# One Trainium2 core: value products of a DMA-turned P one step later, q's products ahead of k's and v's

## The reference

```
q = (x_norm @ Wq.T)   32 heads of 128;   k, v = ctx @ Wk.T, ctx @ Wv.T   8 heads, each used by 4 of q's
q, k = rmsnorm(q) * wq, rmsnorm(k) * wk
scores = q k^T / sqrt(128) + mask;  P = softmax(scores);  out = (P v) @ Wo.T
x = x + tanh(g) * out
```

## Time and profile before

| | us |
|---|---|
| median of 3 runs | 1319.82 (1318.8 to 1320.96) |
| the profiled execution | 1320.3 |
| its span, first to last instruction | 1318.5 |
| TensorE busy in the span | 1302.9 (99%) |
| VectorE busy | 1001.4 (76%) |
| ScalarE busy | 867.4 (66%) |
| GpSimd busy | 621.9 (47%) |

### The profile page before, as it was taken

One profiled execution on the slowest core, in us unless ns is written; L12 is line 12 of the kernel. 1 busy time (PEld: TensorE's weight loads), 2 busy tenths in 40 slices (PEclk: granted clock), 3 DMA queues, 4 the chain that ended last, 5 costly groups with the idle time before them and its releaser, 6 DMA issues.

```text
span 1318.5 us, 25473 instructions
## 1 busy us (share of the span) xinstructions
PE 1302.9 (99%) x7477; PEld 1102.0 (84%) x7493; DVE 1001.4 (76%) x2106; ACT 867.4 (66%) x3356; POOL 621.9 (47%) x683
## 2 busy tenths in 40 slices
PE   8999999999999999999999999999999999999999
PEld 7888888888888888877777788888888888888887
DVE  6878787887878788688888858777767677677656
ACT  5767667676767776645566456777767767676551
POOL 2546566565656666446677533532323323332232
DMA  7011110211121121020301013532232222321101
GB/s 297 1 57 55 63 55 20 68 48 68 50 68 50 35 71 33 13 64 20 103 20 48 20 48 89 161 64 77 60 67 69 40 70 57 80 56 32 17 8 56
DMA packets 87340, 78.34 MB, mean 59 GB/s; under 512 B 70880, under 2 KB 75872, under 8 KB 83168
## 3 DMA queue, kind: packets, MB, share of 16 engines
q1 hardware_dynamic: 70272, 71.91, 18.6%
q10 hardware_dynamic: 16672, 4.46, 1.6%
q0 software_dynamic: 320, 1.05, 0.2%
HBM read 57.48 MB, written 3.15 MB: 46 GB/s over the span
## 4 chain that ended last, share of the span: by engine, by line
PE 76%; issue 8%; POOL 6%; DVE 5%; DMA 3%; ACT 1%; POOLq 0%; ACTq 0%; DVEq 0%; SPq 0%
PE bank L1298 54%; PE bank L1362 6%; PE bank L1290 6%; PE bank L1393 6%; PE bank L1324 2%; DMA p_turned<-p_planes 2%; POOL w_lo L551 2%; POOL rstd L580 2%; PE bank L1479 1%; PE bank L1379 1%; POOL fw_y L591 1%; POOL fw_y L589 1%; DVE probs L1138 1%; ACT squares L769 1%; DMA ctx_raw<-in_ctxT 0%
## 5 line engine op out<-in xcount | busy, mean ns | idle before, releaser
L551 POOL TENSOR_TENSOR w_lo<-w_raw,w_hi (+1 forms) x150 | 192.8, 1303 | 164.7 <-ACT w_hi L730 164.7
L769 ACT ACTIVATE squares<-bank 128x128 bf16<-128x128 f32 x512 | 134.4, 278 | 184.7 <-PE bank L1298 184.5
L711 ACT ACTIVATE probs<-probs,negmax 128x128 f32<-128x128 f32 x512 | 198.2, 391 | 7.1 <-DVE negmax L1010 4.5
L576 POOL TENSOR_TENSOR meansq<-sumsq,scalars 128x5 f32<-128x5 f32 x128 | 27.5, 215 | 354.1 <-ACT squares L769 354.1
L580 POOL TENSOR_TENSOR rstd<-meansq,scalars 128x5 f32<-128x5 f32 x128 | 153.2, 1197 | 10.7 <-POOL meansq L576 1.1
L1298 PE MATMUL bank<-w_hi,oT_hi 128*128 (+1 forms) x512 | 150.9, 416 | 0.0
L1298 PE MATMUL bank<-w_hi,xT_hi 128*128 (+1 forms) x512 | 140.3, 395 | 0.0
L1298 PE MATMUL bank<-w_lo,xT_hi 128*128 (+1 forms) x512 | 138.1, 390 | 0.3
L1362 PEld LDWEIGHTS bank<-kT,qT 128*128 128x128 f32 x1024 | 131.7, 191 | 7.7
L1298 PE MATMUL bank<-w_hi,oT_lo 128*128 (+1 forms) x512 | 138.0, 391 | 0.0
L1298 PE MATMUL bank<-w_lo,oT_hi 128*128 (+1 forms) x512 | 137.6, 390 | 0.0
(11 more groups left out here) (129 smaller groups left out, 3073.1 us busy)
## 6 DMA issues: line engine op xcount, KB each, us to landing
w_raw<-in_wq SPq DMA_DIRECT2D x16, 1024.0 KB, 4.8
w_raw<-in_wo SPq DMA_DIRECT2D x16, 1024.0 KB, 9.8
w_raw<-in_wkv SPq DMA_DIRECT2D x16, 512.0 KB, 5.6
fw_raw<-in_ffn_w SPq DMA_DIRECT2D x36, 192.0 KB, 2.3
x_sb<-in_x SPq DMA_DIRECT2D x7, 256.0 KB, 10.7
ctx_raw<-in_ctxT SPq DMA_DIRECT2D x7, 256.0 KB, 9.7
fw_raw<-in_ffn_w SPq DMA_DIRECT2D x7, 256.0 KB, 2.7
out<-x_sb SPq DMA_DIRECT2D x7, 256.0 KB, 2.0
```

The lines of the kernel that those rows point to most:

```text
L551: last = nc.gpsimd.tensor_tensor(lo, raw, hi.bitcast(FP32), ALU.subtract)
L576: nc.gpsimd.tensor_tensor(meansq[:, :], sumsq[:, :], eps_sb[:, :], ALU.add).then_inc(ms_done, 1)
L711: last = nc.scalar.activation(probs[:, h * P:(h + 1) * P], probs[:, h * P:(h + 1) * P], ACT.Exp, bias=negmax[:, h:h + 1], accum_out=rowsum ...
L769: last = nc.scalar.activation(squares[:, h // 2, (b + 1) % 4, h % 2, :], q_bank(n, kind)[:, h * P:(h + 1) * P], ACT.Square, scale=SCALE, a ...
```

## The change

`values_late` holds for steps 76 to 124. In these:

- TensorE makes q's products first, then the first 4 of the 12 products of k and v, then the value products of unit n-3 (`values(3)`, before: of n-2, behind kn's transpose), then the other 8. q's transposes follow kn's at once. Step 75 has no value products; step 124 has two sets.
- ScalarE squares q before k (into qn as a dump, so it waits for the transposes of the last qn), and writes oT_hi between the two. sq_done, for which GpSimd waits, comes with k's squares. In all steps by DMA, the placing of P's upper half and pT_hi go to the end of the step.
- VectorE makes pT_lo at the head of the next step (`whole_lower`), ahead of the planes; oT_lo comes behind the planes, behind the int4 work of steps 76 to 78, and behind wp_lo, which moves to steps 84 to 87. `place_lower` goes to the end of the step. In step 124 the moments and the normalising of the last layer's first tile come earlier.
- SPLIT_ZONE gives step 81 two pieces (before: three), step 82 two (two), step 83 two (one).

SP's order is unchanged, and on GpSimd only the pieces of steps 81 to 83 move.

The diff, cut to its core:

```diff
-              32: ((E + 1, 6), (E + 1, 7)), 33: ((E + 1, 8), (E + 1, 9), (E + 2, 0)), 34: ((E + 2, 1), (E + 2, 2)),
-              35: ((E + 2, 3),), 36: ((E + 2, 4), (E + 2, 5)), 37: ((E + 2, 6),), 38: ((E + 2, 7), (E + 2, 8)),
+              32: ((E + 1, 6), (E + 1, 7)), 33: ((E + 1, 8), (E + 1, 9)), 34: ((E + 2, 0), (E + 2, 1)),
+              35: ((E + 2, 2), (E + 2, 3)), 36: ((E + 2, 4), (E + 2, 5)), 37: ((E + 2, 6),), 38: ((E + 2, 7), (E + 2, 8)),
...
+        def values_late(n, kind):
+
+            return kind == PLAIN or (isinstance(n, int) and DMA0 < n <= DMA1)
...
+            def q_squares(n, b, kind):
+                act.wait_ge(q_ps, n + 1)
+                wait(act, rs_done, n)
+                if values_late(n, kind):
+                    act.wait_ge(qk_ps, n)
+                for h in range(REP):
...
                 if has(n, 0):
-
+                    if values_late(n, kind):
+                        q_squares(n, b, kind)
+                        output_upper(n)
                     act.wait_ge(kv_ps, n + 1)
...
+            def whole_lower(n):
+
+                dve.wait_ge(pt_hid, n - 2)
+                nc.vector.tensor_tensor(pT_lo[:, :], p_whole[:, :], pT_hi[:, :].bitcast(FP32),
+                                        ALU.subtract).then_inc(pt_lod, 1)
...
+                if by_dma(n, kind) or t.last == 0:
+                    scaled_probs(n)
+                if values_late(n, kind):
+                    whole_lower(n)
                 if by_dma(n, kind):
-                    scaled_probs(n)
                     probs_planes(n)
+                for k in gathered(n - 1, kind):
...
+                if kind == ZONE and 0 <= n - INT4_0 < INT4_PARTS and values_late(n, kind):
+                    int4_weights(n - INT4_0)
+                if values_late(n, kind):
+                    output_lower(n)
...
+                    if values_late(n, kind):
+                        queries()
+                        wait(pe, kT_sb, n)
+                        keys_values(slice(0, KT))
+                        values(3)
+                        keys_values(slice(KT, 3 * KT)).then_inc(kv_ps, 1)
```

More of the change, by code:

```diff
@@ L730, in split_upper, with output_upper @@
                     nc.scalar.activation(hi, raw, ACT.Copy).then_inc(split_hi, 1)
+            def q_squares(n, b, kind):
[4 more added lines that the diff above has]
+                for h in range(REP):
+                    dump = (qn[:, h * P // 2:(h + 1) * P // 2].bitcast(BF16) if values_late(n, kind)
+                            else squares[:, h // 2, (b + 1) % 4, h % 2, :])
+                    last = nc.scalar.activation(dump, q_bank(n, kind)[:, h * P:(h + 1) * P], ACT.Square, scale=SCALE,
+                                                accum_out=sumsq[:, h:h + 1])
+                return last
+            def output_upper(n):
+                act.wait_ge(pv_ps, n - 2)
+                wait(act, y_ps, n - 3)
+                nc.scalar.activation(oT_hi[:, :], psPO[:, :], ACT.Copy).then_inc(o_hid, 1)
             def step(n, b, kind, j, q=None):
@@ L734, in step @@
                 exp_late = calm(n, kind) or (kind == FIRST and b == BATCHES - 1)
[L735 to L739, removed]
+                if has(n, 3) and not values_late(n, kind):
+                    output_upper(n)
                 if calm(n, kind) or (kind == ZONE and n == FFN0):
@@ L764, in step @@
                     hidden_turned(0, t.down)
[L765 to L771, removed]
+                if has(n, 0) and not values_late(n, kind):
+                    q_squares(n, b, kind).then_inc(sq_done, 1)
                 if t.first is not None:
@@ L836, in step @@
                     nc.scalar.activation(qT[:, :], psSQ[:, :], ACT.Copy).then_inc(qT_sb, 1)
+                if has(n, 2) and by_dma(n, kind):
+                    act.wait_ge(pv_ps, n - 2)
+                    act.wait_ge(planes_turned, (n - DMA0 + 1) * 16)
+                    nc.scalar.activation(halves(p_whole[:, :])[:, :, 1], p_turned[:, 0:KT, :].rearrange("p k t -> p (k t)"),
+                                         ACT.Copy).then_inc(upper_placed, 1)
+                    act.wait_ge(upper_placed, n - DMA0 + 2)
+                    act.wait_ge(lower_placed, n - DMA0 + 2)
+                    nc.scalar.activation(pT_hi[:, :], p_whole[:, :], ACT.Copy).then_inc(pt_hid, 1)
                 if has(n, 1) and (t.next is not None or t.down is not None):
@@ L1096, in step @@
                     row_inverse(n)
-                if has(n, 2) and not t.active and not by_dma(n, kind):
+                if has(n, 2) and not t.active and not by_dma(n, kind) and t.last != 0:
                     scaled_probs(n)
@@ L1105, in step @@
                         ctx_lower(t.first)
-                if kind == ZONE and 0 <= n - INT4_0 < INT4_PARTS:
+                if kind == ZONE and 0 <= n - INT4_0 < INT4_PARTS and not values_late(n, kind):
                     int4_weights(n - INT4_0)
[L1108 to L1112, removed]
                 if t.first is not None:
@@ L1115, in step @@
                     normalise(t.first, t.first, f_s[:, :])
-                if t.last is not None:
-                    wait(dve, xT_ps, 2 * BATCHES + t.last if t.last else 0)
-                    normalise(NORM["last", t.last], t.last, f_s[:, :])
+                if t.last is not None and t.last:
+                    last_normalised(t.last)
                 if t.norm is not None:
```

91 lines of the change are left out of this document (49 added, 42 removed).

## The result

Median 1339.62 us (1338.56 to 1340.64, 4 runs), the kernel before 1319.99 us in the same comparison (1318.8 to 1320.96, 4 runs): ratio 1.0151, 95% interval 1.0137 to 1.0164. The forecast was 1326.5, with a range to 1331. The direction was right; the time lies 13 us above the forecast and outside its range.

What follows compares the result with a forecast made beforehand. TensorE bounds the kernel, busy 1302.9 of 1318.5 us. From the profiled 1320.3: -7.5 (waits), +14.0 (unrolled steps), +0.2 (step 124) give 1327.0, as a median 1326.5; range 1313 to 1331.

Steps and rivals of the forecast that it cites:

- the waits for kn and pT_lo, -7.5: TensorE, steps 75 to 123: all waits behind the DMA-turned P go, -7.5 us, bounds 0 and -8.6.
- the steady step: TensorE's undisturbed step: same matmuls in another order, still 9.06 us, so 0, within 0.02 a step.
- contention in the unrolled steps, +14.0: Steps 76 to 87: w_lo starts first and holds VectorE's plane copies, oT_lo comes late; +14.0 us in all.
- The 32 steps of the loop: 0: Loop steps: the first plane copy precedes w_lo, oT_lo is in time; 0 us, bounds 0 and 13.2.
- B: Rival, chance 0.10: w_lo goes first in the loop too, 12 more steps lose 1.1 each; 1339.7 us.
- The sign: Whole kernel: the change makes it slower, chance 0.61, against 0.24 for faster and 0.15 for same.
- C: Rival, chance 0.24: nothing is held, oT_lo is in time everywhere, only the removed waits count; 1312.5 us.
- A: Rival, chance 0.23: plane copies precede w_lo in the unrolled steps too, leaving 9.4 us there; 1321.9 us.

Runs made afterwards that it cites:

- the first run of that kind: Changed kernel without the doubled waits, with GpSimd's w_lo pieces put behind rstd in steps 77 to 87, w_hi left in place: 1313.72 us (0.9958).
- the two runs without holes: Changed kernel with 16 ScalarE instructions (waits) added in steps 49 to 64: 1324.6 us; changed kernel with q_squares' two repeated waits removed: 1325.06 us.
- the wait on GpSimd: Changed kernel without the doubled waits, GpSimd holding the first w_lo piece until pT_lo is written in steps 77 to 87: 1320.66 us (1.0006).
- the run moved by 44: Changed kernel without the doubled waits, with 44 ScalarE instructions (88 waits on a count long reached) added in steps 48 to 69: 1329.14 us (1.007).

## Why the prediction was right or wrong

**Right: the waits for kn and pT_lo, -7.5.** All of them went. With w_lo out of the way (the first run of that kind) the stretch from kn to kn is 446.53 us, 4.9 less than in the earlier trace rows; what is missing from 7.5 is the next point, step 80 (0.56) and some first steps.

**Nearly right: the steady step.** "0, within 0.02 a step" came out as 0.03 to 0.04, since q's and o's products take 2.85 each where I had 2.83: 1.4 us over the 38 steps outside 77 to 87.

**Right mechanism, size off: contention in the unrolled steps, +14.0.** The runs show 110.75 - 99.7 = 11.1 (0.4 of it is the longer steady step), and 0.76 to 0.81 in a step of two pieces where I had 1.1. w_lo started first, as forecast, by 0.03. In step 81 q's first matmul lies at 844.47 (0.47 behind kn); from there the second copy ended at 5.89 and not at 6.23 (847.39 + 2.97 = 850.36): w_lo began at 2.89 where I had 3.02, and w_lo and copies in turn took 3.00 up to there, not 1.29 + 0.33 twice. The loop's 0 for this was right, with the second copy held as forecast. Step 80, which I had counted among them, lost as much (0.82) for another reason: there w_hi came 0.7 to 0.9 late, behind the load of its raw piece, and no copy was held.

With these terms alone the changed kernel takes 1324.6 to 1325.1 us, as the two runs without holes show; the forecast was 1326.5.

**Wrong: "The 32 steps of the loop: 0".** This is the step that put the time outside the range. I bounded it by contention with w_lo alone, and did not ask where the instructions that the change adds push the loop behind them. ScalarE got 55 more instructions up to the loop's start, and 8 more in it (counted in the traces), and without the doubled waits, which are on counts that it had already waited for, all of them are gone again. They moved the loop's body to a place where instructions are loaded anew on each pass, and each of three back-jumps then cost 5.3 us: two holes, 2.9 to 3.1 us from the jump on and 1.8 to 2.1 soon after, less what slack there was, and a lower clock behind the stall. The prediction counted such a cost nowhere. That B's number (1339.7) is the measured one is chance: its mechanism, loop steps of 10.2 in three of eight, did not occur.

**The sign rested on the zone.** C's time of 1312.5, "nothing is held", is what the change gives when w_lo is moved (1313.7). Its condition was named rightly; in the kernel as changed it was not met. A's time of 1321.9, "the copies go first in the unrolled steps too", is near what the wait on GpSimd gives (1320.7), though A's list charges step 84 with 2.1 where the sum has 1.7, without a reason.

## What to carry to other kernels

Where a change adds or takes instructions ahead of a hardware loop, compare the rows just behind the back-jumps of every engine, and the packets of the instruction queues, before and after: a hole whose releaser is "issue" at each pass is not the schedule's, and a few waits more or fewer may move it away. A redundant wait is not free where it lies in an engine's stream ahead of a loop like this one (282 to 290 instructions on ScalarE). And an order that takes the slack out of one engine makes every later disturbance on it count: a first hole of 2.0 to 2.6 us cost under 1 us a jump in the old order and 1.6 in the new, and 5.3 where a second one came with it.

## What was not expected of the hardware

- Behind a back-jump ScalarE goes on at once or stands still for 2.0 to 2.8 us, by the position of the body alone: 50 instructions ahead of the loop bring the hole, 80 take it away. Its instructions come in packets of 8.2 KB.
- The clock behind the stall. Windows of the changed kernel at the first long step (length, busy time and count of TensorE, granted clock, DMA share, GB/s): after 3.83 us of standing still it was granted 0.54 of 2.4 GHz, so near 1.2 GHz, for the next 3.6 us and then rose. In the run moved by 44, after 1.30 us of standing still, it stayed at 1.00.

```profile
992.40:996.40 4.00, 0.21 (x2) 1.00 0.60 157
996.40:1000.00 3.60, 3.55 (x9) 0.54 0.00 0
1000.00:1001.80 1.80, 1.80 (x12) 0.98 0.00 0
```

- Of the 5.67 us that the first long step lost (14.76 - 9.09), 1.58 are this slower clock (o's products, 4.43 for 2.85).
